# Third layer's experts: gate times up is split ahead of the next unit, and the router's weights are spread over two experts

## The reference

```
weights = golden_weights(x, Wr, temperature)       # tokens x 8 experts
gate = einsum('btd,edf->betf', x, Wg)
up   = einsum('btd,edf->betf', x, Wu)
h    = silu(gate) * up
out  = einsum('bte,betd->btd', weights, einsum('betf,efd->betd', h, Wd))
```

## Time and profile before

| | us |
|---|---|
| median of 3 runs | 866.83 (865.06 to 867.51) |
| the profiled execution, its own time | 858.83 |
| its span, first to last instruction | 856.3 |
| PE busy / PEld busy | 838.8 (98%) / 710.0 (83%) |
| DVE / ACT / POOL busy | 631.1 / 472.1 / 455.6 |
| PE's share of the chain that ended last | 85% |

### The profile page before, as it was taken

One profiled execution on the slowest core, in us unless ns is written; L12 is line 12 of the kernel. 1 busy time (PEld: TensorE's weight loads), 2 busy tenths in 40 slices (PEclk: granted clock), 3 DMA queues, 4 the chain that ended last, 5 costly groups with the idle time before them and its releaser, 6 DMA issues.

```text
span 856.3 us, 15659 instructions
## 1 busy us (share of the span) xinstructions
PE 838.8 (98%) x5436; PEld 710.0 (83%) x5436; DVE 631.1 (74%) x1275; ACT 472.1 (55%) x944; POOL 455.6 (53%) x316
## 2 busy tenths in 40 slices
PE   8999999999999999999999999999999999999998
PEld 7888888888856899999999878778888887886688
DVE  6899999999987756655656969577667695345767
ACT  3666666676654566646643375633453425357743
POOL 6676767676614655666666021059718216708720
PEclk9999999999999999999999999999999999999999
DMA  8101010101007275456113050011111010030001
GB/s 335 39 20 37 18 37 18 37 18 37 0 1 273 87 255 202 151 185 206 63 44 96 40 209 1 0 51 50 37 37 37 13 62 1 1 148 3 3 2 50
DMA packets 23342, 62.17 MB, mean 73 GB/s; under 512 B 3136, under 2 KB 13632, under 8 KB 20224
## 3 DMA queue, kind: packets, MB, share of 16 engines
q1 hardware_dynamic: 21760, 57.35, 19.5%
q0 software_dynamic: 1536, 4.20, 1.5%
HBM read 50.00 MB, written 8.39 MB: 68 GB/s over the span
## 4 chain that ended last, share of the span: by engine, by line
PE 85%; DVE 8%; ACT 2%; POOL 2%; issue 1%; DMA 1%; SPq 0%; DVEq 0%; ACTq 0%; POOLq 0%
PE banks L102 25%; PE banks L104 24%; PE banks L103 24%; PE banks L1344 3%; DVE banks L1875 1%; PE banks L1330 1%; POOL arenaB L841 1%; POOL arenaC L841 1%; DVE arenaC_rounded L1884 1%; PE banks L999 1%; PE banks L1171 1%; PE banks L934 1%; PE banks L933 1%; PE banks L1013 1%; PE banks L854 1%
## 5 line engine op out<-in xcount | busy, mean ns | idle before, releaser
L2079 ACT ACTIVATE banks<-banks,small 128x512 f32<-128x512 f32 x128 | 84.9, 663 | 74.2 <-DVE small L1480 74.2
L1480 DVE TENSOR_REDUCE small<-banks 128x1 f32<-128x512 f32 x128 | 87.1, 680 | 4.9 <-PE banks L104 4.9
L104 PE MATMUL banks<-arenaC_rounded,arenaD_rounded 128*128 128x512 f32 (+1 forms) x256 | 89.4, 349 | 0.0
L102 PE MATMUL banks<-xnT_rounded,arenaD_rounded 128*128 128x512 f32 x224 | 88.1, 393 | 1.3 <-POOL arenaC_rounded L721 1.0
L103 PE MATMUL banks<-s_tok_rounded,arenaD_rounded 128*128 128x512 f32 x224 | 88.0, 393 | 0.0
L104 PE MATMUL banks<-xnT_rounded,arenaD_rounded 128*128 128x512 f32 x192 | 75.1, 391 | 0.0
L104 PE MATMUL banks<-xnT_rounded,arenaC_rounded 128*128 128x512 f32 x192 | 74.8, 390 | 0.0
L102 PE MATMUL banks<-arenaC_rounded 128*128 128x512 f32 (+1 forms) x192 | 70.9, 369 | 1.1 <-DVE arenaC_rounded L1633 0.6
L1495 DVE SCALAR_TENSOR_TENSOR arenaC<-banks,small,arenaC 128x512 f32<-128x512 f32 x96 | 71.4, 744 | 0.0
L103 PE MATMUL banks<-arenaD_rounded,arenaC_rounded 128*128 128x512 f32 (+1 forms) x192 | 68.0, 354 | 0.0
L707 POOL TENSOR_TENSOR arenaD_rounded<-arenaC,ones 128x512 fp32r<-128x512 f32 x30 | 31.2, 1040 | 49.6 <-DVE arenaC L1495 48.6
(11 more groups left out here) (431 smaller groups left out, 2728.8 us busy)
## 6 DMA issues: line engine op xcount, KB each, us to landing
arenaD<-in_wexp SPq DMA_DIRECT2D x8, 1060.0 KB, 6.7
arenaD<-in_wexp SPq DMA_DIRECT2D x8, 1024.0 KB, 4.9
arenaC<-in_wqkv SPq DMA_DIRECT2D x16, 384.0 KB, 3.0
arenaD<-in_wexp SPq DMA_DIRECT2D x8, 512.0 KB, 3.5
slots<-arenaB SPq DMA_DIRECT2D x1, 2560.0 KB, 10.6
arenaB<-in_sw SPq DMA_DIRECT2D x1, 2084.0 KB, 7.5
arenaC<-in_wo SPq DMA_DIRECT2D x1, 2048.0 KB, 15.5
arenaC<-slots SPq DMA_DIRECT2D x8, 256.0 KB, 3.4
```

Of the source, the lines that this page charges most:

```text
L102: pe.matmul(o, r(lhs[0]), r(rhs[0]), start=start, stop=False)
L104: return pe.matmul(o, r(lhs[1]), r(rhs[0]), start=False, stop=stop)
L1480: dve.tensor_reduce(negmax[:, n % 4:n % 4 + 1], bank[3 + n % 4][:, :], AX.X, ALU.max, negate=True).then_inc(max_done, 1)
L2079: act.activation(prob[r], prob[r], ACT.Exp, bias=negmax[:, r:r + 1], accum_out=rowsum[:, r:r + 1]).then_inc(exp_done, 1)
```

## The change

It moves instructions; no arithmetic is added or taken away. On VectorE `rest_gu` of a unit follows its own `mult` instead of the next one, and on ScalarE `round_gu` follows the unit's own silu. ScalarE's two gate/up copies stand in units 1 and 2, one each, and the down copy in unit 3, all before that unit's `round_gu`. `down_rest(e)` goes from the tail of `following(e - 1)` into `following(e)`, between mult 1 and rest 1 of expert e + 1. The router's chain is cut in eight parts: four behind the mults of expert 0, four behind those of expert 1; `gold_done` comes after the last. `following(0)` and `following(1)` are written out ahead of the loop on VectorE.

```diff
+            def golden_part(e, n):
+
+                if (e, n) == (0, 0):
+                    golden_zone()
+                elif (e, n) in ((0, 1), (0, 3)):
+                    golden_find()
+                elif (e, n) in ((0, 2), (1, 0)):
+                    golden_mark(e)
+                elif (e, n) == (1, 1):
+                    golden_normal(fb)
+                elif (e, n) == (1, 2):
+                    golden_mix()
+                else:
+                    golden_normal(gw)
...
                     dve.tensor_tensor(v, v, gs[n % 2], ALU.mult).then_inc(gu_done, 1)
-                    if n:
-                        rest_gu(e, q, n - 1)
-                    if n == 3:
-                        rest_gu(e, q, n)
...
                 for n in range(4):
                     mult(0, 0, n)
-                    golden_parts[n]()
-                dve.sem_inc(gold_done, 1)
+                    golden_part(0, n)
+                    rest_gu(0, 0, n)
                 def following(e, q, between=None):
 
                     for n in range(4):
                         mult(e + 1, 1 - q, n)
+                        if isinstance(e, int) and e == 0:
+                            golden_part(1, n)
+                            if n == 3:
+                                dve.sem_inc(gold_done, 1)
+                        elif n == 1:
+                            down_rest(e, q)
+                        rest_gu(e + 1, 1 - q, n)
                         if between and n == 1:
                             between()
                     gateup_rest(e + 2, q)
-                    down_rest(e + 1, 1 - q)
                     add_expert(e, q)
 
-                with dve.Fori(0, E2 // 2 - 2) as pair:
+                following(0, 0)
+                following(1, 1)
+                with dve.Fori(1, E2 // 2 - 2) as pair:
...
                     for n in range(4):
-                        silu_round(e + 1, 1 - q, n)
-                        if n == 1:
-
-                            round_gateup(e + 2, q, turn + 1)
-                        if n == 2:
-
+                        silu2(e + 1, n)
+                        if n in (1, 2):
+                            round_gateup(e + 2, q, turn + 1, (n - 1,))
+                        if n == 3:
                             round_down(e + 1, 1 - q, turn + q)
+                        round_gu(e + 1, 1 - q, n)
```

More of the change, by code:

```diff
@@ L1748, in golden_zone, with golden_find @@
                 link(dve.memset(mask2, 0.0))
-            def golden_pick(k):
+            def golden_find():
                 link(dve.tensor_reduce(red8[:, 2, :], cand, AX.X, ALU.max))
@@ L1755, in golden_pick, with golden_mark @@
                 link(dve.tensor_reduce(red8[:, 3, :], zone, AX.X, ALU.min))
+            def golden_mark(k):
                 link(dve.tensor_tensor(zone, iota, per(red8[:, 3, :]), ALU.is_equal))
@@ L1760, in golden_pick, with golden_normal, golden_mix @@
                     link(dve.tensor_tensor(fb, fb, mask2, ALU.mult))
[L1762 to L1770, removed]
+            def golden_normal(v):
+                link(dve.tensor_reduce(red8[:, 4, :], v, AX.X, ALU.add))
+                link(dve.tensor_scalar(red8[:, 4, :], red8[:, 4, :], 1e-8, None, ALU.max))
+                link(dve.reciprocal(red8[:, 4, :], red8[:, 4, :]))
+                link(dve.tensor_tensor(v, v, per(red8[:, 4, :]), ALU.mult))
+            def golden_mix():
                 link(dve.tensor_tensor(fb, fb, per(red8[:, 1, :]), ALU.mult))
@@ L1774, in golden_weights @@
                 link(dve.tensor_tensor(gw, gw, fb, ALU.add))
-                normal(gw)
-            golden_parts = [golden_zone, lambda: golden_pick(0), lambda: golden_pick(1), golden_weights]
+            def golden_part(e, n):
[11 more added lines that the diff above has]
+                    golden_normal(gw)
             def residuals(layer, b, between=None):
@@ L1928, in _ @@
                     mult(E2 - 1, 1, n)
+                    if n == 1:
+                        down_rest(E2 - 2, 0)
+                    rest_gu(E2 - 1, 1, n)
                 down_rest(E2 - 1, 1)
@@ L2301, in _, with round_gateup @@
                 act.sem_inc(silu2_done, 2)
-                def round_gateup(e, q, turn):
+                def round_gateup(e, q, turn, which=range(2)):
                     act.wait_ge(w2exp_in[q], 16 * turn + 16)
-                    for i in range(2):
+                    for i in which:
                         act.copy(r(wexp2_hi[q][:, i]), wexp2[q][:, i]).then_inc(gateup_rounded, 1)
@@ L2336, in round_gu @@
                     act.copy(r(gu_hi[q][:, n // 2, n % 2 * S:(n % 2 + 1) * S]), bank[2 + n % 2][:, :]).then_inc(gu_rounded, 1)
[L2338 to L2343, removed]
                 for n in range(4):
-                    silu_round(0, 0, n)
+                    silu2(0, n)
+                    round_gu(0, 0, n)
                 def following(e, q, turn):
                     for n in range(4):
-                        silu_round(e + 1, 1 - q, n)
-                        if n == 1:
-                            round_gateup(e + 2, q, turn + 1)
-                        if n == 2:
+                        silu2(e + 1, n)
+                        if n in (1, 2):
+                            round_gateup(e + 2, q, turn + 1, (n - 1,))
+                        if n == 3:
                             round_down(e + 1, 1 - q, turn + q)
+                        round_gu(e + 1, 1 - q, n)
                 with act.Fori(0, E2 // 2 - 2) as pair:
@@ L2365, in _ @@
                 for n in range(4):
-                    silu_round(E2 - 1, 1, n)
+                    silu2(E2 - 1, n)
                     if n == 2:
                         round_down(E2 - 1, 1, E2 // 2 - 1)
+                    round_gu(E2 - 1, 1, n)
                 if layers > 3:
```

## The result

The changed kernel took 853.99 us in the median of four runs (853.51 to 856.89), the kernel before 865.94 (860.07 to 867.51) on the same occasion: ratio 0.990, 95% interval 0.9867 to 0.9934 (the two medians alone would give 0.986). Faster was forecast and came true; the time of 861.0 and its range of 859.2 to 864.6 did not. On two later occasions the ratio was 0.9925 (0.991 to 0.9939) and 0.9922 (0.9909 to 0.9934), and the kernel before read 857.8 and 857.9. So the saving was forecast nearly right (5.8; the stage gives 6.3), and the level that it was taken from was not.

What follows compares the result with a forecast made beforehand. TensorE bounds the kernel, losing 7.4 us in gaps before up products. Of this 6.3 is won, less 0.3 (`down_rest`) and 0.2 (expert 5): 5.8 off the median 866.83 gives 861.0, range 859.2 to 864.6.

Steps and rivals of the forecast that it cites:

- TensorE is the bound, and the loss is in the starts of its matmuls: Third layer's experts: 17 gaps before up products, where TensorE waits for `rest_gu`, cost 7.4 us; 6.3 can be won.
- The subtraction ahead of the next unit: VectorE runs `rest_gu` directly after its own `mult`, ending at T + 2.6, before TensorE wants the bank at T + 4.3.
- The slack: Time between the subtraction's end and TensorE's need of its bank: 1.7 us, where 0.2 to 0.3 was short.
- Expert 0: Its first gap of 1.77 us loses 0.60 and 1.05 stays; its other gap and those of expert 1 close.
- The later router: Router's chain runs into expert 1, so GpSimd starts near 572.4, some 7 us later, inside its idle time: nothing charged.
- `down_rest`: Moved between mult 1 and rest 1, it may delay up 3 beside GpSimd: 0 to 1.6 us, 0.3 charged.
- Expert 5's start: After ScalarE's table load, silu 1 stands behind round 0: a gap of 0 to 0.5 us stays, 0.2 charged.
- The step that failed: Whole kernel's level: the 5.8 us saving was taken from the median of 866.83, giving 861.0, not from the profiled 858.83.
- A: Rival: GpSimd's exclusions also delay `gateup_rest` in three or four experts, losing 1.5 to 3.5 us: 863.3; chance 0.19.
- C: Rival: `down_rest` between mult 1 and rest 1 holds up 3's bank, making the kernel slower, 869.1 us; chance 0.04.
- B: Rival: the gaps are the semaphore's own cost, not VectorE's order; only expert 0's 0.60 us is won, 866.2; chance 0.04.

Runs made afterwards that it cites:

- `vector_order`: The changed kernel with ScalarE in the order of before (silu n, then round n - 1; both weight copies behind unit 1): ratio to before 0.9925.
- `scores_early`: The changed kernel with GpSimd's rotary scores released ahead of the router's chain instead of behind it: 866.54 us, ratio to before 1.0115.
- `down_at_tail`: The changed kernel with `down_rest` back at the end of `following`, ahead of `add_expert`: ratio to before 0.993.
- `router_only`: The kernel before with only the router's chain cut in eight parts over experts 0 and 1: ratio to before 0.9997.

## Why the prediction was right in its mechanism and wrong in its time

- *TensorE is the bound, and the loss is in the starts of its matmuls.* Right. The stage lost 6.33 us (128.88 to 122.55), where 6.3 were to be won and 5.8 were left after charges. The gaps alone account for 5.85: 7.4 before, less 1.05 and 0.50 after. The other 0.5 lies in the matmuls behind each restart: without the gaps and the 0.34 behind them, the 512-column matmuls of the stage start 0.2289 us apart in before's trace and 0.2274 in the changed one's, which over 321 of them is 0.5. The restart cost a little more than the 0.11 that I had added.
- *The subtraction ahead of the next unit.* Right: it starts 1.36 us after its mult, and no product but the two named waits for it. The slack is real: ScalarE's old order, worked out to take 1.2 of its 1.7 us, brings no gap back by itself. The mults start 0.43 us after the last matmul of up, not 0.53, most likely because they no longer stand in a loop (last section).
- *Expert 0.* Right: 1.17 in place of 1.77; its other gap and the three of expert 1 closed.
- *The later router.* GpSimd began at 573.69, or 572.0 less the 1.65 us that this trace was late already; 572.4 was forecast. I charged nothing, as nobody waits for GpSimd's scores. True, but I asked only who waits for GpSimd, not whom its operations hold up where they now lie: that made the gap at expert 5.
- *`down_rest`.* 0.3 was charged, nothing was paid in the changed kernel, 0.4 once in `vector_order`.
- *Expert 5's start.* 0.2 of 0 to 0.5 was charged and 0.50 paid, for the reason just given and not for silu 1's place behind round 0.
- *The step that failed* was none of these, but the level that the saving was taken from: "The median of the runs shown is 866.83, 8.0 above it; the same 5.8 gives 861.0." On three further occasions 75 timed executions of before lay between 856.1 and 860.4, with medians of 857.3 to 858.1. The profiled execution's 858.83 was the kernel's level and the three timed runs were not. Counted from it the forecast was 853.0, and the profiled execution of the changed kernel took 854.03; the 1.0 between them is chance, 0.5 more won in the stage and 1.5 lost in the gaps at 466 to 469 us. An 8 us step between a profile and three timed runs is three times what a measurement tells from no change. I took it for a constant and let the unknowns of the stage alone set the range, where the step itself should have been one of its ends.
- *Rivals.* A and C did not come in the changed kernel, and each shows once in `vector_order`, at 0.4 us with the restart. A's own loss of 1.5 to 3.5 us would have given 862.5 to 864.5, not up to 865. B is out as the cause of the gaps; only 0.06 to 0.09 us of each of the six gaps in experts 2 to 4 did not come from the order (last section).

What stays open is why before's first four timed runs read 860 to 867.5. A lower clock could make such a step: `scores_early` took 865.9 us at 0.995 and 870.7 at 0.987, that is 0.6 us for each 0.001. But it was not seen for before below 0.995, and those four runs have neither a trace nor a clock on record. The changed kernel's four runs of that occasion have a clock, and they speak against it as the only cause: 853.5 to 856.9 us at 0.997, where later runs took 851.7 to 851.9 at 0.997 and 0.998. In the one that was traced the gaps marked issue, at full clock, make 1.5 us of the excess. Whether the same lengthened the runs of before is not known.

## What to carry to other kernels

When two engines work on a unit in turn and the next unit can't be ready sooner anyway, let each finish its part first: what frees the buffer then stands at the head of the queue, and waiting for the other engine costs nothing. Look for the loss in the starts of the bounding engine's instructions and in its weight loads' waits: a busy share of 98% hid 6 us here. And settle the level that a forecast starts from: where a profiled execution lies 1% off the timed ones, put both levels into the range; here only one of them held.

## What the runs showed of the hardware

- A wait costs more than itself: the matmul behind the first starts 0.34 instead of 0.23 us later at every gap at full clock, even after one of 0.1 us, and once (`down_at_tail`, 599.01 us) without any gap ahead.
- The granted clock explains most of the scatter: at 1.000, 0.998 and 0.995 the kernel before takes some 856.5, 858.1 and 859.8 us. A long wait can have the lower clock behind it. In `scores_early` TensorE had waited 4.85 us between two matmuls at 552.6, and 2.23 us at 565.1; the stretches behind:

```profile
557.00:561.00 4.00, 3.58 (x9) 2.84 (x10) 3.93 (x5) 1.09 (x2) 3.84 (x3) 0.57 0.00 0
...
568.00:572.00 4.00, 4.00 (x12) 3.12 (x11) 3.86 (x7) 1.62 (x3) 3.73 (x4) 0.60 0.02 4
```

  Matmuls started 0.43 us apart there, so these two gaps were paid again, at 0.2 us a matmul, 3.3 us in all. But the length of the wait alone does not decide: behind a wait of 3.12 us at 586.8 in the same trace the clock stayed up, and so it did behind the gaps of 0.8 to 1.8 us in expert 0 in the other traces.

```profile
589.90 0.49 PE L102 MATMUL banks<-xnT_rounded,arenaB_rounded 128*128 128x512 f32 x1 [2.84 <-DVE arenaD_rounded L1873]
590.23 0.39 PE L103 MATMUL banks<-s_tok_rounded,arenaB_rounded 128*128 128x512 f32 x1
590.46 0.40 PE L104 MATMUL banks<-xnT_rounded,arenaD_rounded 128*128 128x512 f32 x1
```

- In the kernel before the same gap is 0.50 in the rounds of the loops and 0.39 to 0.41 where the code is written out (602.51 and 675.17). In `router_only` it is 0.41 in experts 2 to 7. The difference sits in the start of VectorE's mult. Expert 3 in before (its mult 1 is at 601.67), then in `router_only`:

```profile
601.15 0.39 PE L104 MATMUL banks<-xnT_rounded,arenaD_rounded 128*128 128x512 f32 x1
```

```profile
600.02 0.39 PE L104 MATMUL banks<-xnT_rounded,arenaD_rounded 128*128 128x512 f32 x1
600.45 0.70 DVE L1890 TENSOR_TENSOR banks<-banks,arenaC 128x512 f32<-128x512 f32 x1 [1.10 <-PE banks L104]
```

  That is 0.52 after the last matmul of up against 0.43. Units 1 to 3 of experts 2 to 4 in before have 0.51 to 0.52, those of experts 5 to 7 have 0.43, as all of these have in `router_only`. Ahead of these mults before's trace has register operations of 0.04 us on VectorE's queue (ALU_OP, L1873). In `router_only` the loop has one round left, and its trace has none there. So the loop's register operations are the likely cause of the 0.09 us. No run changed the loop alone.
